# Values of the attention by two half-height matmuls per head, in banks of their own

## The chip, the cores and the metric

The kernel runs on one core of a Trainium2 chip. The metric is the device time of one execution in microseconds (us). A core has TensorE (matrix products, results into PSUM, eight banks of 128 partitions by 512 fp32), VectorE, ScalarE, GpSimd and SyncE (here it only issues DMAs). Each engine runs its own instruction stream in order, and streams wait for each other by semaphores.

## The reference

A decoder layer over x, 16 batches of 64 tokens, 256 wide: layernorm and self-attention, layernorm and cross attention, layernorm and a mixture of experts, each added to x. What matters here is the self-attention, with 16 heads of 128:

```
w = codes * repeat(scales, 32, axis=0)          # for q, k, v and the output
q, k, v = x @ wq + bq, x @ wk + bk, x @ wv + bv  # each (16, 64, 16 heads, 128)
scores  = einsum('bqhd,bkhd->bhqk', q, k) / sqrt(128)
attn    = softmax(scores)
out     = einsum('bhqk,bkhd->bqhd', attn, v) @ wo + bo
```

A batch attends only to itself: 64 queries on 64 keys.

## The kernel before

The 1024 tokens are eight tiles of 128, two batches each. The attention goes through eight head groups c (0 to 7): four heads at a time (hq = c % 4), for four tiles (g = c // 4). `stage_order` writes out one list of steps, `ORDER`, and each engine's program walks it and does its part of each step, so the order on every engine is fixed by hand.

For a head group:

- `scores(c)`: products of 64 queries by 64 keys, into banks 2 and 3. Their stationary operand has 64 columns and the two batches of a tile land in different halves of the partitions (L434).
- `qk(c + 1, h)` for four heads: two results of four matmuls each (L404), q drained by ScalarE, k also by ScalarE but for head 3, which VectorE drains (kT, L914). Between them ScalarE takes the exponential (L724) and VectorE maximum, sums and the product with the inverse sums, which writes the probabilities `Pb`, in a block-diagonal form: batch 0 of a tile in rows and columns 0 to 63, batch 1 in 64 to 127, zeros elsewhere.
- Then for tiles i = 0 to 3, woven into each other: `turn(c, i)` transposes the probabilities of four heads (L447), ScalarE copies them to `PT` (L734); `v(c + 1, i)` makes the V of the next group (L417), drained by ScalarE or VectorE in turns; `values(c, i)` multiplies V and PT (L455); ScalarE copies the result as `OTh` (fp32r, L739), VectorE writes the rest, `OTl` (L965); `outs(c, i)` multiplies both with wo into banks 6 and 7 (L468). The order of TensorE is turn 0, turn 1, v 0, values 0, turn 2, values 1, v 1, outs 0, turn 3, values 2, v 2, outs 1, values 3, v 3, outs 2, outs 3.

After some groups other steps follow: the context's transposes (L478) after group 0, bias and the query-key blocks (L488, L498) after group 3, four transposes of the normalized x and the output blocks (L391 and L392, L509) after group 4. Group 7 has no V of a next group: in its place stand the query weights (`query_weights(m)`, two heads each, L519), drained by ScalarE (`Ah`, L762) and then VectorE (`Al`, L986). The cross attention starts with `rotate(0, 0)` (L534).

Results other than scores and outs take their bank from a ring: `take` gives the next of banks 0, 1, 4, 5 (`ring`, L371) and waits until the last result there is drained. So turn, v, qk, values, context, blocks and query weights share four banks, in the order of TensorE. A values result `pv` is drained by the OTl instruction, and `Banks` keeps a pair of semaphores per bank, full and drained. An fp32 matmul shows as two records in the trace, each with a weight load of its own; one of fp32r or a transpose as one record.

Of the kernel before, what the change touches and what calls it, by code (L numbers as in the profile page):

```python
# [7 lines left out]
ALU = mybir.AluOpType  # L8
ACT = mybir.ActivationFunctionType
# [198 lines left out]
def f32(ap):  # L208
    return ap.bitcast(F)
# [7 lines left out]
def program(nc, x, codes, scl, woc, wos, bq, bk, bv, bo, tabs, cks, tri, kvc, wqr, wkr, kckv, wot, wqx,  # L217
            kcq, wg, w13, w2, out):
    with ExitStack() as ctx:
        def sem(name):  # L220
            return ctx.enter_context(nc.semaphore(name))
# [90 lines left out]
        V = at("V", R3 + 16384, [128, 4, 512])  # L312
        Pb = at("Pb", R3 + 24576, [128, 16, 128])
        PT = [at(f"PT{i}", R3 + 32768 + 2048 * i, [128, 512]) for i in range(2)]
        OTh = [at(f"OTh{i}", R3 + 36864 + 2048 * i, [128, 512], R) for i in range(2)]
        OTl = [at(f"OTl{i}", R3 + 40960 + 2048 * i, [128, 512], R) for i in range(2)]
# [11 lines left out]
        psum = nc.alloc_psum_tensor("psum", [128, 4096], F)  # L328
        ps = Banks(psum, sem)
        y_bank = (4, 5, 6, 7)  # L330

        s_zero, s_ident, s_half, s_kvz, s_pbz = (sem(n) for n in ("zero", "ident", "half", "kv_zero", "pb_zero"))
        d_x, d_cst, d_kvr = [sem("x0_in"), sem("x1_in")], sem("const_in"), sem("kv_in")
# [11 lines left out]
        s_mx, s_exp, s_sum, s_rs = sem("row_max"), sem("exp"), sem("row_sum"), sem("row_inverse")  # L345
        s_pb, s_pb_pool = sem("probs"), sem("probs_by_pool")
        s_ot_hi, s_outs, s_x2, s_xb = sem("ot_hi"), sem("outs"), sem("x2"), sem("x_bias")
        s_kvt, s_kv2 = sem("kv_turned"), sem("kv2")
        s_bv, s_aw_hi = sem("bv_split"), sem("aw_hi")
        s_tt, s_rp_lo, s_rp_hi, s_rp_hi_pool = sem("tt"), sem("rp_lo"), sem("rp_hi"), sem("rp_hi_by_pool")  # L350
# [2 lines left out]
        s_gate, s_route, s_rexp, s_pad = sem("gate"), sem("route"), sem("route_exp"), sem("pad")  # L353
        s_comb = sem("combine")
        s_sl, s_sl2, s_gt_hi, s_down, s_y = sem("silu"), sem("silu2"), sem("gt_hi"), sem("down"), sem("y")

        def wqk(hq, h):
            return (s_wqk_dve, 1 + (h >= 2)) if hq == 0 else (s_wqk_dve, 3) if hq == 1 else (s_wqk_pool, hq - 1)
# [9 lines left out]
        def tensor_program():  # L368
            te = Engine(nc.tensor)
            pe = nc.tensor  # L370
            ring = [0, 0, (0, 1, 4, 5)]  # L371

            def take(*name):
                b = ring[2][ring[0] % len(ring[2])]
                ring[0] += 1
                if b >= 6:
                    te.wait_ge(s_x2, 8)
                ap, n = ps.place(b, *name)
                te.wait_ge(ps.drained[b], n)
                return b, ap  # L380
# [67 lines left out]
                mm.then_inc(ps.full[b], 1)  # L448

            def values(c, i):  # L450
                b, ap = take("pv", c, i)
                te.wait_ge(*ps.emptied("turn", c, i))
                te.wait_ge(*ps.emptied("v", c, i))
                for h in range(4):
                    mm = pe.matmul(ap[:, 128 * h:128 * h + 128], V[:, i, 128 * h:128 * h + 128],  # L455
                                   PT[i % 2][:, 128 * h:128 * h + 128], start=True, stop=True)
                mm.then_inc(ps.full[b], 1)

            def outs(c, i):
                hq = c % 4  # L460
                te.wait_ge(*ps.emptied("pv", c, i))
                te.wait_ge(*wo_(hq))
                if c == 4:
                    te.wait_ge(s_x2, 2 * (i // 2) + 2)
                dst = ps.ap[6 + i // 2][:, 256 * (i % 2):256 * (i % 2) + 256]
                for h in range(4):
                    for n, part in enumerate((OTh, OTl)):
                        mm = pe.matmul(dst, part[i % 2][:, 128 * h:128 * h + 128], wo[:, 4 * hq + h, :],  # L468
                                       start=(hq == 0 and h == 0 and n == 0 and i % 2 == 0),
                                       stop=(hq == 3 and h == 3 and n == 1), skip_group_check=True)  # L470
                mm.then_inc(s_outs, 1)
# [49 lines left out]
                    mm.then_inc(ps.full[b], 1)  # L521

            def rotate(g, j):
                if (g, j) == (0, 4):
                    ring[2] = (0, 1, 4, 5, 6, 7)
                te.wait_ge(*ps.emptied("aw", 15))
                for i in range(4):
                    te.wait_ge(*ps.emptied("xT", 1, 4 * g + i))
                both = take("rot", g, j, 0), take("rot", g, j, 1)
                for half_, (b, ap) in enumerate(both):  # L530
                    n = 0
                    for kt in range(2):
                        for w, xp in ((Ah, xTh), (Ah, xTl), (Al, xTh)):
                            mm = pe.matmul(ap, w[:, kt, half_, 128 * j:128 * j + 128],  # L534
                                           xp[:, kt, 512 * g:512 * g + 512], start=(n == 0), stop=(n == 5))
                            n += 1
                    mm.then_inc(ps.full[b], 1)
# [143 lines left out]
        def scalar_program():  # L681
            sc_ = Engine(nc.scalar)
            act = nc.scalar.activation
# [29 lines left out]
            def v_out(c, i):  # L713
                if i % 2 == 0:
                    sc_.wait_ge(*ps.filled("v", c, i))
                    if c > 0:
                        sc_.wait_ge(*ps.filled("pv", c - 1, i))
                    act(V[:, i, :], ps.of("v", c, i), ACT.Copy).then_inc(ps.drain("v", c, i), 1)

            def exp(c):  # L720
# [5 lines left out]
            def turn(c, i):  # L726
                sc_.wait_ge(*ps.filled("turn", c, i))
                if c == 0:
                    sc_.wait_ge(s_kv2, 2)
                if i >= 2:  # L730
                    sc_.wait_ge(*ps.filled("pv", c, i - 2))
                elif c > 0:
                    sc_.wait_ge(*ps.filled("pv", c - 1, i + 2))
                act(PT[i % 2][:, :], ps.of("turn", c, i), ACT.Copy).then_inc(ps.drain("turn", c, i), 1)  # L734

            def values(c, i):
                sc_.wait_ge(*ps.filled("pv", c, i))
                sc_.wait_ge(s_outs, 4 * c + i - 1)
                act(OTh[i % 2][:, :], ps.of("pv", c, i), ACT.Copy).then_inc(s_ot_hi, 1)  # L739

            def context_turn():
                for q in range(4):
# [108 lines left out]
        def vector_program():  # L851
            ve = Engine(nc.vector)
            tt_, ts_, red = nc.vector.tensor_tensor, nc.vector.tensor_scalar, nc.vector.tensor_reduce
# [63 lines left out]
            def v_out(c, i):  # L917
                if i % 2 == 1:
                    ve.wait_ge(*ps.filled("v", c, i))
                    if c > 0:  # L920
                        ve.wait_ge(*ps.filled("pv", c - 1, i))
                    copy(V[:, i, :], ps.of("v", c, i)).then_inc(ps.drain("v", c, i), 1)

            def less_max(k, *name):
# [37 lines left out]

            def values(c, i):
                ve.wait_ge(s_ot_hi, 4 * c + i + 1)
                tt_(OTl[i % 2][:, :], ps.of("pv", c, i), f32(OTh[i % 2][:, :]),  # L965
                    ALU.subtract).then_inc(ps.drain("pv", c, i), 1)

            def bias():
                ve.wait_ge(d_cst, 96)
# [20 lines left out]
            def rotate(g, j):  # L990
                k = 12 * g + j
                lo, hi = ps.of("rot", g, j, 0), ps.of("rot", g, j, 1)
# [4 lines left out]

                ve.wait_ge(d_cst, 96)
                if k == 0:
                    for i in range(4):  # L1000
                        ve.wait_ge(*ps.filled("pv", 7, i))
                ve.wait_ge(*ps.filled("rot", g, j, 0))
                ve.wait_ge(s_rp_lo, k)
                times(0, lo)
# [442 lines left out]
```

## Time and profile before

| | |
|---|---|
| median of 3 runs | 750.25 us (748.35 to 751.52) |
| profiled execution, its own time | 744.96 us |
| its span | 743.7 us |
| granted TensorE clock, mean | 0.988 |
| TensorE busy | 693.1 us, 93% |
| VectorE busy | 411.5 us, 55% |
| ScalarE busy | 261.5 us, 35% |
| GpSimd busy | 171.3 us, 23% |
| values (L455) on TensorE | 256 records of 276 ns |

A record's duration is longer than its place in the stream, as matmuls are pipelined; what a matmul takes of the engine is read from the distance between starts. The self-attention fills the first 256 us of the span. PE is TensorE's matmul part, PEld its weight loads, DVE VectorE, ACT ScalarE, POOL GpSimd. A granted clock of 1.00 is 2.4 GHz, 0.50 is 1.2 GHz.

### The profile page before, as it was taken

The page shows a single profiled execution, that of the slowest core. Times are in us where ns is not written, and L with a number is a line of the kernel's source. Part 1 is how long each engine was busy: PE and PEld are TensorE (multiplying, and loading weights), DVE is VectorE, ACT ScalarE, POOL GpSimd, SP SyncE. Part 2 cuts the span into 40 slices and gives each one's busy share as a digit, 9 for nine tenths or more (in the row PEclk, how much of TensorE's full clock was granted, in tenths as well). Part 3 has the DMA queues.
Part 4 walks back from the last instruction along what each step waited for, and adds up shares of the span by engine and source line. Part 5 has one row for each costly group of instructions (what it writes and reads, how often), then busy time and mean ns, then how long its engine had stood idle before and what let it go on. Part 6 is the DMA issues. An engine that isn't in the chain of part 4 may idle for free.

```text
span 743.7 us, 11108 instructions
## 1 busy us (share of the span) xinstructions
PE 693.1 (93%) x4516; PEld 602.5 (81%) x4516; DVE 411.5 (55%) x801; ACT 261.5 (35%) x522; POOL 171.3 (23%) x111
## 2 busy tenths in 40 slices
PE   7889899999998999989999968969879999999998
PEld 6778788988887956657667667868769999999997
DVE  3377575273455586765475387675575444434344
ACT  1254354353543401030221232432453453443432
POOL 3536030210001032233241312211322241220200
PEclk9999999999999999999999989999999999999999
DMA  8999030032001200000000022101110311100001
GB/s 270 256 242 244 13 142 2 1 149 77 32 2 49 90 0 1 0 1 1 0 1 1 9 112 81 61 18 44 61 48 27 108 61 61 61 1 1 1 1 58
DMA packets 13764, 44.39 MB, mean 60 GB/s; under 512 B 2193, under 2 KB 2705, under 8 KB 13457
## 3 DMA queue, kind: packets, MB, share of 16 engines
q1 hardware_dynamic: 12704, 42.54, 19.0%
q10 hardware_dynamic: 1008, 1.14, 0.5%
q8 instruction: 36, 0.59, 0.3%
q14 instruction: 16, 0.12, 0.1%
HBM read 42.62 MB, written 1.05 MB: 59 GB/s over the span
## 4 chain that ended last, share of the span: by engine, by line
PE 77%; DVE 14%; DMA 4%; issue 2%; ACT 2%; POOL 1%; SPq 1%; DVEq 0%
PE psum L634 18%; PE psum L662 9%; PE psum L534 7%; PE psum L552 7%; PE psum L404 4%; PE psum L468 4%; PE psum L455 4%; PE psum L596 4%; DMA sclB<-in_scl 4%; PE psum L567 3%; PE psum L417 3%; PE psum L646 3%; PE psum L434 3%; DVE Pb L959 2%; DVE sm L1039 2%
## 5 line engine op out<-in xcount | busy, mean ns | idle before, releaser
L634 PE MATMUL psum<-w13h,xTh 128*128 128x352 f32 x288 | 96.1, 334 | 0.0
L634 PE MATMUL psum<-w13h,xTl 128*128 128x352 f32 x288 | 94.5, 328 | 0.0
L634 PE MATMUL psum<-w13l,xTh 128*128 128x352 f32 x288 | 94.2, 327 | 0.0
L1138 DVE SCALAR_TENSOR_TENSOR gg<-sl,comb,psum 128x176 f32<-128x176 f32 x104 | 41.2, 397 | 83.9 <-ACT sl L833 83.7
L1246 POOL TENSOR_TENSOR w13l<-w13r,w13h 128x1408 fp32r<-128x1408 f32 x13 | 41.8, 3214 | 167.0 <-ACT w13h L816 167.0
L995 DVE TENSOR_TENSOR tt<-psum,tab 128x512 f32<-128x512 f32 x96 | 60.6, 682 | 26.3 <-PE psum L534 25.4
L833 ACT ACTIVATE sl<-psum 128x176 f32<-128x176 f32 x112 | 35.5, 318 | 112.5 <-PE psum L634 112.4
L662 PE MATMUL psum<-w2h,gTh 128*128 128x256 f32 x216 | 67.4, 312 | 6.7 <-DVE gTl L1144 5.6
L662 PE MATMUL psum<-w2h,gTl 128*128 128x256 f32 x216 | 61.3, 284 | 0.0
L662 PE MATMUL psum<-w2l,gTh 128*128 128x256 f32 x216 | 61.3, 284 | 0.0
L552 PE MATMUL psum<-rp,Mb 128*128 128x512 f32 x128 | 58.0, 597 | 0.4 <-DVE rp L1020 0.3
L634 PEld LDWEIGHTS psum<-w13h,xTh 128*128 128x128 f32 x288 | 55.6, 193 | 0.8 <-issue 0.8
L404 PE MATMUL psum<-xTh,W 128*128 128x512 f32 x128 | 52.2, 408 | 4.1 <-DVE W L895 4.0
L634 PEld LDWEIGHTS psum<-w13h,xTl 128*128 128x128 f32 x288 | 55.5, 193 | 0.0
L634 PEld LDWEIGHTS psum<-w13l,xTh 128*128 128x128 f32 x288 | 55.2, 192 | 0.3 <-issue 0.2
L1144 DVE TENSOR_TENSOR gTl<-psum,gTh 128x384 fp32r<-128x384 f32 x72 | 40.0, 556 | 24.7 <-ACT gTh L838 20.8
L1239 POOL TENSOR_TENSOR rp<-tt,tt 128x512 f32<-128x512 f32 x24 | 30.7, 1279 | 96.4 <-DVE tt L995 96.4
L965 DVE TENSOR_TENSOR OTl<-psum,OTh 128x512 fp32r<-128x512 f32 x32 | 22.1, 691 | 53.3 <-ACT OTh L739 53.3
L404 PE MATMUL psum<-xTl,W 128*128 128x512 f32 x128 | 51.2, 400 | 0.0
L662 PEld LDWEIGHTS psum<-w2h,gTh 128*128 128x128 f32 x216 | 41.6, 193 | 7.6 <-DVE gTl L1144 6.3
L552 PEld LDWEIGHTS psum<-rp,Mb 128*128 128x128 f32 x128 | 23.6, 189 | 26.7 <-issue 26.3
L534 PE MATMUL psum<-xTh,Ah 128*128 128x512 f32 x96 | 42.3, 440 | 2.0 <-DVE tt L995 2.0
(156 smaller groups left out, 1525.6 us busy)
## 6 DMA issues: line engine op xcount, KB each, us to landing
w13r<-in_w SPq DMA_DIRECT2D x13, 704.0 KB, 4.1
w2r<-in_w SPq DMA_DIRECT2D x13, 384.0 KB, 3.7
raw<-in_codes SPq DMA_DIRECT2D x4, 1024.0 KB, 18.2
sclB<-in_scl SPq DMA_DIRECT2D x16, 256.0 KB, 10.7
raw<-in_codes SPq DMA_DIRECT2D x4, 512.0 KB, 15.6
sclB<-in_scl SPq DMA_DIRECT2D x16, 128.0 KB, 12.9
wor<-in_woc SPq DMA_DIRECT2D x4, 512.0 KB, 10.8
wob<-in_wos SPq DMA_DIRECT2D x16, 128.0 KB, 12.2
```

The lines of the kernel that those rows point to most:

```text
L404: mm = pe.matmul(ap, W[:, kt, m, 512 * hq + 128 * h:512 * hq + 128 * h + 128], xp[:, kt, 512 * g:512 * g + 512], start=(n == 0), stop=(n = ...
L455: mm = pe.matmul(ap[:, 128 * h:128 * h + 128], V[:, i, 128 * h:128 * h + 128], PT[i % 2][:, 128 * h:128 * h + 128], start=True, stop=True)
L534: mm = pe.matmul(ap, w[:, kt, half_, 128 * j:128 * j + 128], xp[:, kt, 512 * g:512 * g + 512], start=(n == 0), stop=(n == 5))
L552: mm = pe.matmul(ap, Mb[:, 4 * hp + 2 * kk + half_, :], rp[(j0 + kk) % 3][:, half_, :], start=(n == 0), stop=(n == 3))
L634: mm = pe.matmul(ap[:, 0:352], xp[:, kt, 128 * t:128 * t + 128], w[q % 2][:, kt, 352 * u:352 * u + 352], start=(k == 0), stop=(k == 5))
L662: mm = pe.matmul(dst, gp[n % 2][:, 128 * c:128 * c + 128], w[q % 2][:, c, :], start=(n == FIRST_Y[t // 2] and k == 0), stop=(q == LAST_Q[t ...
L833: act(sl[n % 2][:, u, :], src, ACT.Silu).then_inc(s_sl, 1)
L995: return tt_(b3(tt[n][:, :], 64), b3(src, 64), tab[:, j % 3, n, :].unsqueeze(1).to_broadcast([128, 8, 64]), ALU.mult)
L1138: op = stt(out=dst, in0=part_, scalar=(combh if n < 16 else comb)[:, t, e:e + 1], in1=b[:, 176:352], op0=ALU.mult, op1=ALU.mult)
L1144: tt_(gTl[n % 2][:, :], ps.of("gt", n)[:, 0:384], f32(gTh[n % 2][:, :]), ALU.subtract).then_inc(ps.drain("gt", n), 1)
L1239: tt_(o[:, 0, :], tt[0][:, :], tt[1][:, :], ALU.subtract).then_inc(s_rp_lo, 1)
L1246: tt_(w13l[q % 2][:, :, :], w13r[q % 2][:, :, :], f32(w13h[q % 2][:, :, :]), ALU.subtract).then_inc(s_w13, 1)
```

## The change

Each head's product of V and PT is split by batch. As PT is block-diagonal, batch 0 needs only rows 0 to 63 of both operands and columns 0 to 63 of PT, batch 1 the other halves. The new `values` issues for each head two matmuls with 64 rows, 128 stationary columns and 64 moving columns, batch 0 on the upper half of the array's rows into bank 4, batch 1 on the lower half into bank 5: 8 matmuls a tile instead of 4. The four heads of a batch lie side by side in 256 columns of its bank.

Banks 4 and 5 are kept for this. The ring is (0, 1) from the start, and becomes (0, 1, 4, 5) at `rotate(0, 0)`, after all values are drained. Two new semaphores take over for the values: `s_pv` (a tile's values are there) and `s_otl` (its OTl is written). `values(c, i)` waits until the OTl of the tile before is written. OTh and OTl are as before one instruction of 512 elements a partition, which read both banks (`pv_out`) and write in the order head, batch, token (`by_head`).

```diff
+        pv_out = psum[:, 2048:3072].rearrange("p (b c) -> p b c", c=512)[:, :, 0:256].rearrange(
+            "p b (h s) -> p h b s", s=64)
...
+        s_pv, s_otl = sem("values"), sem("ot_lo")
...
+        def by_head(ot):
+            return ot[:, :].rearrange("p (h b s) -> p h b s", b=2, s=64)
...
-            ring = [0, 0, (0, 1, 4, 5)]
+            ring = [0, 0, (0, 1)]
...
             def values(c, i):
-                b, ap = take("pv", c, i)
+                te.wait_ge(s_otl, 4 * c + i)
                 te.wait_ge(*ps.emptied("turn", c, i))
                 te.wait_ge(*ps.emptied("v", c, i))
                 for h in range(4):
-                    mm = pe.matmul(ap[:, 128 * h:128 * h + 128], V[:, i, 128 * h:128 * h + 128],
-                                   PT[i % 2][:, 128 * h:128 * h + 128], start=True, stop=True)
-                mm.then_inc(ps.full[b], 1)
+                    for b in range(2):
+                        lo = 64 * b
+                        mm = pe.matmul(ps.ap[4 + b][:, 64 * h:64 * h + 64], V[lo:lo + 64, i, 128 * h:128 * h + 128],
+                                       PT[i % 2][lo:lo + 64, 128 * h + lo:128 * h + lo + 64], start=True, stop=True)
+                mm.then_inc(s_pv, 1)

             def outs(c, i):
                 hq = c % 4
-                te.wait_ge(*ps.emptied("pv", c, i))
+                te.wait_ge(s_otl, 4 * c + i + 1)
...
             def rotate(g, j):
+                if (g, j) == (0, 0):
+                    ring[2] = (0, 1, 4, 5)
+                    te.wait_ge(s_otl, 32)
...
             def values(c, i):            # ScalarE
-                sc_.wait_ge(*ps.filled("pv", c, i))
+                sc_.wait_ge(s_pv, 4 * c + i + 1)
                 sc_.wait_ge(s_outs, 4 * c + i - 1)
-                act(OTh[i % 2][:, :], ps.of("pv", c, i), ACT.Copy).then_inc(s_ot_hi, 1)
+                act(by_head(OTh[i % 2]), pv_out, ACT.Copy).then_inc(s_ot_hi, 1)
...
             def values(c, i):            # VectorE
                 ve.wait_ge(s_ot_hi, 4 * c + i + 1)
-                tt_(OTl[i % 2][:, :], ps.of("pv", c, i), f32(OTh[i % 2][:, :]),
-                    ALU.subtract).then_inc(ps.drain("pv", c, i), 1)
+                tt_(by_head(OTl[i % 2]), pv_out, f32(by_head(OTh[i % 2])), ALU.subtract).then_inc(s_otl, 1)
```

The other waits on `pv` (of PT's and V's copies, which may not overwrite what a values matmul still reads, and of the first rotate on VectorE) become waits on `s_pv` with the count that stands for the same tile.

## Rows read from the trace of the kernel before

**Rows 1.** Page, part 1: busy time of each engine, share of span, instructions.
```profile
PE 693.1 (93%) x4516; PEld 602.5 (81%) x4516; DVE 411.5 (55%) x801; ACT 261.5 (35%) x522; POOL 171.3 (23%) x111
```

**Rows 2.** Windows: stretch, length, busy us by engine, clock; groups 3 and 7.
```profile
116.20:140.40 24.20, 24.20 (x194) 21.96 (x194) 12.92 (x23) 11.63 (x21) 0.00 (x0) 1.00 0.00 1
228.60:256.30 27.70, 24.09 (x209) 23.16 (x209) 16.48 (x30) 13.23 (x26) 3.09 (x2) 1.00 0.19 67
```

**Rows 3.** Timeline of TensorE, group 3: start, duration, engine, line, operation, idle before.
```profile
127.37 1.04 PE L447 MATMUL psum<-ident,Pb 128*128 128x128 f32 x8
128.16 0.48 PE L417 MATMUL psum<-W,xTh 128*128 128x512 f32 x1
...
129.18 1.05 PE L455 MATMUL psum<-PT,V 128*128 128x128 f32 x8
130.07 0.60 PE L447 MATMUL psum<-ident,Pb 128*128 128x128 f32 x4
130.51 1.06 PE L455 MATMUL psum<-PT,V 128*128 128x128 f32 x8
131.41 0.50 PE L417 MATMUL psum<-W,xTh 128*128 128x512 f32 x1
```

**Rows 4.** Waits of TensorE, 20 to 256 us: total, times, longest.
```profile
PE psum L455 <- DVE kT L914: 3.4, 3, 2.1
```

**Rows 5.** Timeline of TensorE around scores, group 3's start and group 4's end.
```profile
116.01 0.27 PE L392 MATMUL psum<-ident,xh 128*128 128x128 f32 x1
116.21 0.50 PE L434 MATMUL psum<-kT,qT 128*64 128x64 f32 x5
...
154.61 0.40 PE L434 MATMUL psum<-kT,qT 128*64 128x64 f32 x4
154.94 0.51 PE L404 MATMUL psum<-xTh,W 128*128 128x512 f32 x1
155.28 0.40 PE L404 MATMUL psum<-xTl,W 128*128 128x512 f32 x1
155.52 0.40 PE L404 MATMUL psum<-xTh,W 128*128 128x512 f32 x1
```

**Rows 6.** Timeline of TensorE's weight loads behind the scores of group 4.
```profile
154.94 0.19 PEld L404 LDWEIGHTS psum<-xTh,W 128*128 128x128 f32 x1
155.04 0.19 PEld L404 LDWEIGHTS psum<-xTl,W 128*128 128x128 f32 x1
```

**Rows 7.** Timeline after group 4: output blocks and next scores; VectorE's xTl.
```profile
176.70 3.67 PE L509 MATMUL psum<-Fo,Fk 128*64 128x256 f32 x32 [0.28 <-DVE xTl L884]
180.21 0.28 PE L434 MATMUL psum<-kT,qT 128*64 128x64 f32 x2
...
176.22 1.41 DVE L884 TENSOR_TENSOR xTl<-psum,xTh 128x256 fp32r<-128x256 f32 x4 [1.57 <-ACT xTh L697]
```

**Rows 8.** Timelines of VectorE and ScalarE beside rows 3.
```profile
128.06 0.75 DVE L914 TENSOR_SCALAR kT<-psum,bks 128x512 f32<-128x512 f32 x1
130.90 0.69 DVE L965 TENSOR_TENSOR OTl<-psum,OTh 128x512 fp32r<-128x512 f32 x1 [2.09 <-ACT OTh L739]
...
130.27 0.60 ACT L739 ACTIVATE OTh<-psum 128x512 fp32r<-128x512 f32 x1 [1.18 <-PE psum L455]
```

**Rows 9.** Timeline of ScalarE, group 4: the third result of qk drained.
```profile
158.73 0.68 ACT L706 ACTIVATE qT<-psum,bqs 128x512 f32<-128x512 f32 x1
```

**Rows 10.** Timelines in group 7: TensorE, then VectorE (from 226 us).
```profile
240.02 1.57 PE L519 MATMUL psum<-Akc,Aq 128*128 128x192 f32 x8 [2.47 <-DVE Al L986]
241.42 1.04 PE L447 MATMUL psum<-ident,Pb 128*128 128x128 f32 x8
...
239.42 3.29 DVE L986 TENSOR_TENSOR Al<-psum,Ah 128x384 fp32r<-128x384 f32 x6
```

**Rows 11.** Windows of the cross attention: clock behind a stretch of idle TensorE.
```profile
433.00:439.70 6.70, 3.02 (x20) 2.76 (x20) 5.08 (x11) 3.93 (x8) 2.00 (x1) 1.00 0.01 3
439.70:446.50 6.80, 4.96 (x19) 4.99 (x20) 6.46 (x18) 1.41 (x3) 1.15 (x1) 0.50 0.01 4
```

More of the change, by code:

```diff
@@ L716, in v_out @@
                     if c > 0:
-                        sc_.wait_ge(*ps.filled("pv", c - 1, i))
+                        sc_.wait_ge(s_pv, 4 * c + i - 3)
                     act(V[:, i, :], ps.of("v", c, i), ACT.Copy).then_inc(ps.drain("v", c, i), 1)
@@ L730, in turn @@
                 if i >= 2:
-                    sc_.wait_ge(*ps.filled("pv", c, i - 2))
+                    sc_.wait_ge(s_pv, 4 * c + i - 1)
                 elif c > 0:
-                    sc_.wait_ge(*ps.filled("pv", c - 1, i + 2))
+                    sc_.wait_ge(s_pv, 4 * c + i - 1)
                 act(PT[i % 2][:, :], ps.of("turn", c, i), ACT.Copy).then_inc(ps.drain("turn", c, i), 1)
             def values(c, i):
-                sc_.wait_ge(*ps.filled("pv", c, i))
+                sc_.wait_ge(s_pv, 4 * c + i + 1)
                 sc_.wait_ge(s_outs, 4 * c + i - 1)
-                act(OTh[i % 2][:, :], ps.of("pv", c, i), ACT.Copy).then_inc(s_ot_hi, 1)
+                act(by_head(OTh[i % 2]), pv_out, ACT.Copy).then_inc(s_ot_hi, 1)
             def context_turn():
@@ L920, in v_out @@
                     if c > 0:
-                        ve.wait_ge(*ps.filled("pv", c - 1, i))
+                        ve.wait_ge(s_pv, 4 * c + i - 3)
                     copy(V[:, i, :], ps.of("v", c, i)).then_inc(ps.drain("v", c, i), 1)
@@ L999, in rotate @@
                 if k == 0:
-                    for i in range(4):
-                        ve.wait_ge(*ps.filled("pv", 7, i))
+                    ve.wait_ge(s_pv, 32)
                 ve.wait_ge(*ps.filled("rot", g, j, 0))
```

## The prediction

> **What bounds the kernel now.** I read the engine table of the page first: TensorE is busy 693 of 743.7 us, and no other engine comes to 60% [rows 1]. An average hides stages, so I cut the attention into the stretches between two score stages. In the stretch of head group 3 TensorE is busy for the whole 24.20 us, VectorE for half of it; in the last stretch (group 7, with the query weights) it is busy 24.09 of 27.70 us and VectorE and ScalarE set the pace [rows 2]. So what TensorE must do or wait for in groups 0 to 6 is path, nearly without cover. Third, the order of TensorE's own work around the change: turns, V, values, turn, values, V, each starting where the last one stops [rows 3]. Fourth, what it waits for: the values wait 3.4 us in 3 groups for kT, which shares their ring bank [rows 4].
>
> **The change, part by part.**
>
> *The matmuls.* Before, a tile takes 8 records of values (4 fp32 matmuls, two records each): 130.51 to 131.41, 0.90 us, or 112 ns each [rows 3]. After, there are 8 matmuls, 16 records, each with half the rows and 64 moving columns instead of 128. What a record costs is the larger of its weight load and its moving pass. The scores stream 64 columns at a spacing of 57 ns (the four last records of the stretch) [rows 5]. A load of 128 columns that finds the array free is followed by the next after 0.10 us [rows 6]. The new load still has 128 columns, so a record can't go below some 0.108 us, unless two loads run at once. Whether two of them on different halves of the rows do, no row shows. The nearest rows are the output blocks, whose matmuls alternate between two halves of the columns: 32 records of 256 moving columns in 3.51 us, 0.22 us a pair [rows 7]; alone, such a record would take twice the 0.108 us that 128 fp32 columns take. So pairs overlap fully there, loads too. I take the same for halves of the rows: 8 pairs of 0.108 us are 0.86 us against 0.90, a gain of 0.03 x 32 tiles = 1.0 us. The other end is no overlap, 16 x 0.108 = 1.73 us, a loss of 0.83 x 32 = 26.6 us. The best end is a pair in the time of a scores record, 8 x 0.057 = 0.46 us, a gain of 0.44 x 32 = 14 us.
> The Trainium skill ("TensorE: Matmul & The Clock Gate", LDWEIGHTS) says that a load's time goes by its columns and not by the rows in use; by that rule, halving the rows saves nothing, and only overlap keeps the loads from doubling.
>
> *Entering and leaving the split array.* Around the scores, the only matmuls of half width in this stage, the trace shows what a change of shape costs. Into it: 0.20 us between starts (116.01 to 116.21) where such transposes follow at 0.11 [rows 5], 0.09 more. Out of it: from the last record (154.61 + 3 x 0.057 = 154.78) to 154.94 is 0.16 us against 0.057, 0.10 more; then 0.34 against 0.235 until the next, 0.10 more, because its load could not be made ahead [rows 5, 6]. Going in, the first 128-column load is bare as well, 0.10. An excursion so costs 0.39 us; the old values paid at most 0.1 of such a gap, and not everywhere; I take 0.38. Bounds: 0 if splitting rows is free, 0.4 if as here. Each of 32 tiles is one excursion: 25 in full (9.5 us); in groups 0 to 6 the first tile pays only 0.09, as its way out lies inside the wait costed below (0.6 us). Together 10.1 us.
> The Trainium skill ("TensorEngine Tiling (Array Packing)", Key Properties) states that changing the tiling mode, not just the tile, drains TensorE. The trace agrees in sign, with the 0.09 and 0.10 us above; this rule speaks against the change.
>
> *The ring of two banks.* Banks 4 and 5 leave the ring, so from the start to the first rotate a result goes to bank 0 or 1 and must be drained before the second next.
> - kT and the second turn. The order is ..., q of head 3, k of head 3, turn 0, turn 1: turn 1 now takes kT's bank, where before it was the first values, after V. kT is drained by VectorE behind the probabilities, at 128.06 + 0.75 = 128.81 [rows 8]. Turn 1 starts at 128.87, then 0.44 us of transposes and 1.02 of V (128.16 to 129.18 [rows 3]): values start at 130.33 instead of 129.18, 1.15 late, in four groups (3 to 6). In groups 0 to 2 the old values already waited for kT [rows 4], so nothing of turn 1 and V (0.44 + 0.94) is covered any more: 1.4 each. 4 x 1.15 + 3 x 1.4 = 8.8 us. Queued behind the waiting turn on TensorE are V and the values, and ScalarE and VectorE wait for these.
> - q and k of the next group: groups of 4 matmuls each 0.93 us. ScalarE drains in 0.69 and just keeps up, but it holds the third result until both exponentials are out (158.73 + 0.68 = 159.41 [rows 9]), and TensorE would write that bank at 154.94 + 4 x 0.93 = 158.66: 0.75 late. 0.45 of it disappears in the wait for kT; 0.3 x 4 groups = 1.2 us. (Groups 0 to 2 are bound by kT anyway.)
> - Elsewhere: context turn, the four xT turns (xTl alone takes VectorE 1.41 us [rows 7], and a third turn waits for the first xTl) and the output and key blocks. 2.0 us, between 0 and 4.
>
> *The values' own banks.* The values of tile i+1 wait for OTl of tile i. In group 3, OTl is done at 130.90 + 0.69 = 131.59, 2.41 us after its values began [rows 3, 8]; with a bare load and a semaphore's way 2.55. The second values began 1.33 us after the first (129.18 to 130.51). So 1.2 us of wait, in 7 groups: 8.4 us. Tiles 2 and 3 come 2.8 us or more after the one before and just escape. In group 7 query weights lie between the first two, and this wait is nothing.
>
> *Group 7.* Query weights take a bank per head. Before, four results fit ahead of the probabilities; now two, and each later pair waits for Al. VectorE runs six Al from 239.42 in one go while TensorE resumes at 240.02 [rows 10]; with two banks TensorE, ScalarE and VectorE take turns, some 1.1 to 2 us a pair, and turn 0 waits for the seventh Al: by my count at 244.05 instead of 241.42, 2.6 late, and turn 2 another 0.7. 3.3 us, bounds 1 and 5.
>
> *The clock.* A stretch in which TensorE was busy 3.02 of 6.70 us was followed by one at half clock (0.50, the 1.2 GHz level) for 6.80 us [rows 11]. The idle places of group 7 now come near that. I add 1.7 us (3.4 us at half rate); bounds 0 and 3.4.
>
> *ScalarE's and VectorE's copies* keep 512 elements a row and one instruction each (0.60 and 0.69 us [rows 8]); read over two banks in runs of 64 I cost them at nothing, bounds 0 and 0.1 us each.
>
> *Sum.* -1.0 + 10.1 + 8.8 + 1.2 + 2.0 + 8.4 + 3.3 + 1.7 = 34.5 us. Groups 0 to 2 run beside the loads of weights and GpSimd's products, and a later TensorE finds these further on: I take 2 us off (0 to 4). That is 32.5 us on the profiled execution's own 744.96 us, 777.5. The runs shown have a median of 750.25, 5.3 above that one; on it, the same difference gives 782.8, and I say 782.
>
> **The rivals.**
> - *The halves don't overlap* (the change does not do what it says). Speaking for it: no row has two row halves; against: the column halves. The tile takes 1.73 us instead of 0.86, on the path: 27.6 us more, 810.
> - *Cheap split.* Rows split without a change of shape, and the waits partly covered: without the 10.1 us and with 4 us less of ring waits, 768. Against it: the scores' rows.
> - *Faster.* A pair goes at the pace of the scores, 0.057 us, at 14 us gained, shapes change free, and the ring's waits of groups 0 to 2 fall into weight loads. It begins where the tile's gain exceeds the waits: with 14 gained, no more than 10 may remain of the 25.4 us of waits (8.8 + 1.2 + 2.0 + 8.4 + 3.3 and 1.7 of clock). At 10 left the time is 746. Against it: the spacing of bare loads [rows 6] and TensorE without a gap to hide in [rows 2].
> - *No change*, a mixture of these near 750.
>
> **How the numbers follow.** Forecast 0.65, no overlap 0.17, cheap split 0.10, faster 0.04, no change 0.04. 0.5% (3.8 us) is about what a measurement tells from none. Faster 0.04, same 0.04, slower 0.92. The likeliest case has its own range of 770 to 795; the range is 765 to 812, which takes in no overlap and nearly all of the cheap split.
>
> **What would show it.** Right: 16 records of values per tile, starting within some 10 ns of each other two by two, 0.11 us a pair; 0.09 us and more around them; a new wait of the turns (L447) for kT of 1 us a group; a new wait of the values for OTl of about 1 us, once a group; stretches of groups 3, 5 and 6 near 28 us instead of 24.2; nothing changed from the rotates on. Wrong: values of 1.7 us (no overlap) or 0.5 us (loads faster than the bare ones); no wait for OTl, which would mean that the ring had been the limit before; or ScalarE's copy well above 0.60 us.

## The result, and the profile after

The changed kernel takes 779.95 us (median of 4 runs, 775.17 to 785.03) against 749.74 us of the kernel before beside it: a ratio of 1.040, 95% interval 1.033 to 1.048. The forecast was 782, within 765 to 812. The profiled execution took 775.17 us with a span of 773.9, 30.2 us more than the one of before.

The page's first part, answering to [rows 1]: TensorE has 20 us more to do by its own records, and 10 us more in which it stands still.

```profile
PE 713.2 (92%) x4772; PEld 603.8 (78%) x4772; DVE 409.1 (53%) x801; ACT 265.4 (34%) x522; POOL 171.4 (22%) x111
```

Windows of the kernel after, answering to [rows 2]: the start up to the first scores, group 5 (as group 3, but with no blocks behind it), group 7, and the stretch of half clock in it. Columns: stretch, length, busy us of PE, PEld, DVE, ACT, POOL, clock, DMA.

```profile
0.00:32.10 32.10, 25.22 (x116) 19.92 (x116) 12.74 (x26) 8.78 (x14) 17.72 (x18) 0.89 0.96 262
196.99:224.87 27.88, 26.36 (x226) 21.62 (x223) 11.90 (x19) 12.01 (x20) 0.00 (x0) 1.00 0.20 72
252.83:286.40 33.57, 27.42 (x241) 24.58 (x241) 17.04 (x30) 13.67 (x26) 3.09 (x2) 0.95 0.16 55
265.60:269.00 3.40, 2.92 (x10) 2.42 (x8) 1.58 (x3) 1.06 (x3) 0.00 (x0) 0.50 0.04 14
```

TensorE no longer fills group 5: 27.88 us, 1.52 of them idle, where it had 24.18 without a gap. The rest, from the first rotate on, takes 487.4 us against 487.3: the whole difference lies in the self-attention.

TensorE in group 3, answering to [rows 3]. Here transposes are L453, V L423, values L463.

```profile
136.12 0.66 PE L453 MATMUL psum<-ident,Pb 128*128 128x128 f32 x4
137.10 0.66 PE L453 MATMUL psum<-ident,Pb 128*128 128x128 f32 x4 [0.33 <-DVE kT L925]
137.51 0.48 PE L423 MATMUL psum<-W,xTh 128*128 128x512 f32 x1
...
138.62 1.11 PE L463 MATMUL psum<-PT,V 64*128 64x64 f32 x16
139.66 0.66 PE L453 MATMUL psum<-ident,Pb 128*128 128x128 f32 x4
141.15 1.11 PE L463 MATMUL psum<-PT,V 64*128 64x64 f32 x16 [0.84 <-DVE OTl L976]
142.19 0.50 PE L423 MATMUL psum<-W,xTh 128*128 128x512 f32 x1
142.53 0.40 PE L423 MATMUL psum<-W,xTl 128*128 128x512 f32 x1
```

Sixteen records take 1.04 us up to the next V where eight took 0.90. The pairs are real. A window of 0.1 us at the second values holds two weight loads and two matmuls, each pair merged into one row that begins at 141.15:

```profile
141.15 0.19 PEld L463 LDWEIGHTS psum<-PT,V 64*128 64x128 f32 x2 [1.07 <-DVE OTl L976]
```
```profile
141.15 0.33 PE L463 MATMUL psum<-PT,V 64*128 64x64 f32 x2 [0.84 <-DVE OTl L976]
```

In the trace's nanoseconds the two starts are 7 apart, the next pair comes 160 later (its load was bare) and each further pair 112 after the last: as much as one full-height record before. So the pairs gained nothing at all, and the change of shape is paid on top. The first part of the price stands in the stage that follows: the first record of V starts 0.20 us after the last pair, where before it came 0.12 us after the last record. The two places where the path stands still are also in these rows: turn 1 waits for kT, the second values for OTl.

The waits of TensorE up to 290 us, answering to [rows 4] (total, times, longest):

```profile
PE psum L463 <- DVE OTl L976: 5.8, 7, 0.8
PE psum L527 <- DVE Al L996: 5.0, 3, 2.5
PE psum L410 <- ACT qT L717: 4.7, 7, 1.7
PE psum L410 <- DVE W L906: 3.7, 1, 3.7
PE psum L453 <- DVE kT L925: 2.8, 7, 0.7
PE psum L397 <- DVE xTl L895: 1.6, 2, 0.9
```

Seven waits for OTl (one a group, not in group 7), seven for qT in the matmuls of q and k, and seven for kT. Why kT is late shows in VectorE's row beside the ones of group 3: it begins 0.55 us after VectorE was free, on the release of a matmul of k. It is the filling that is late, not VectorE. The second row is the OTl that ends at 141.10; the second values start 0.05 us later.

```profile
136.30 0.75 DVE L925 TENSOR_SCALAR kT<-psum,bks 128x512 f32<-128x512 f32 x1 [0.55 <-PE psum L410]
140.41 0.69 DVE L976 TENSOR_TENSOR OTl<-psum,OTh 128x512 fp32r<-128x512 f32 x1 [3.36 <-ACT OTh L750]
```

Group 7, answering to [rows 10]: the query weights come two heads at a time, each time behind Al, and turn 0 starts at 269.14, 16.3 us after its scores instead of 12.8 (241.42 after 228.61).

```profile
260.20 1.57 PE L527 MATMUL psum<-Akc,Aq 128*128 128x192 f32 x8 [2.10 <-DVE Al L996]
264.24 1.61 PE L527 MATMUL psum<-Akc,Aq 128*128 128x192 f32 x8 [2.46 <-DVE Al L996]
266.33 2.88 PE L527 MATMUL psum<-Akc,Aq 128*128 128x192 f32 x8 [0.48 <-DVE Al L996]
269.14 0.66 PE L453 MATMUL psum<-ident,Pb 128*128 128x128 f32 x4
```

The lengths below are worked out from the starts of the score stages in the timelines (group 7 up to the first rotate), in us. They carry most of what follows: groups 5 and 6 hold nothing but the attention, away from weight loads, and where neither has a star they agree to 0.1 us. A star marks a stretch with 3.4 us or more of half clock in it.

| kernel | before scores | 0 | 1 | 2 | 3 | 4 | 5 | 6 | 7 |
|---|---|---|---|---|---|---|---|---|---|
| before | 29.35* | 32.58 | 28.74 | 25.55 | 35.03 | 28.96 | 24.18 | 24.23 | 27.73 |
| after | 32.10* | 33.27 | 28.79 | 29.77 | 38.97 | 34.09 | 27.88 | 27.96 | 33.60* |
| ring_only | 32.51* | 30.72 | 32.83* | 27.64 | 36.88 | 32.01 | 25.82 | 25.84 | 32.24* |
| ring_and_one_bank | 35.20* | 32.34 | 32.45* | 28.79 | 38.02 | 33.12 | 26.93 | 26.98 | 32.58* |
| halves_two_pairs | 32.78* | 33.10 | 32.82* | 28.87 | 38.06 | 33.21 | 26.97 | 27.01 | 33.64* |
| halves_ring4 | 29.19* | 32.26 | 26.75 | 27.14 | 37.11 | 31.04 | 26.26 | 26.31 | 28.82 |
| full_height_64 | 33.02* | 35.86 | 30.94 | 32.32 | 41.52 | 38.19* | 30.46 | 30.49 | 34.80 |
| halves_in_order | 33.77* | 34.45 | 31.95* | 33.24* | 42.47* | 36.08 | 31.39* | 33.00* | 35.49* |
| kt_by_scalare | 29.22 | 39.50* | 28.47 | 31.39* | 39.03 | 34.11 | 27.91 | 27.99 | 32.40 |
| exp_later | 29.33* | 39.48* | 28.50 | 28.55 | 40.59* | 34.18 | 27.99 | 29.55* | 33.38* |
| full_banks23 | 29.40* | 32.03* | 29.23* | 24.96 | 34.92 | 28.85 | 24.07 | 24.12 | 28.96* |
| banks23_kt_by_scalare | 27.93 | 33.58* | 26.95 | 24.93 | 34.92 | 28.85 | 24.07 | 24.13 | 27.72 |

The 2.75 us by which the stretch ahead of the first scores grew are mostly not the change's. VectorE dequantizes the first weights W when their scales have landed (the row's wait for `sclB`), before and after:

```profile
14.29 2.36 DVE L895 TENSOR_TENSOR W<-raw,sclB 128x1024 fp32r<-128x1024 f32 x2 [3.44 <-DMA sclB<-in_scl]
16.19 2.36 DVE L906 TENSOR_TENSOR W<-raw,sclB 128x1024 fp32r<-128x1024 f32 x2 [4.71 <-DMA sclB<-in_scl]
```

The load came 1.90 us later in this execution, and the first matmul of q starts 1.90 us later with it (17.56 against 15.66); ring_only, with the same ring, has this row at 14.27. The change doesn't touch these loads. The stretch also holds 3.4 us more of half clock, some 1.7 us at half rate.

### The profile page after: what moved, and what is told of

The parts are those of the page before. It is cut to its first block, busy times and chain, and to the rows that moved or that the text cites. A ratio compares the mean times of both kernels' runs of the same rounds, so it can differ in the third digit from the quotient of the medians.

```text
span 773.9 us, 11618 instructions
## 1 busy us (share of the span) xinstructions
PE 713.2 (92%) x4772; PEld 603.8 (78%) x4772; DVE 409.1 (53%) x801; ACT 265.4 (34%) x522; POOL 171.4 (22%) x111
## 4 chain that ended last, share of the span: by engine, by line
PE 78%; DVE 11%; ACT 4%; DMA 4%; issue 2%; POOL 1%; SPq 0%; DVEq 0%
PE psum L645 17%; PE psum L673 9%; PE psum L563 7%; PE psum L545 7%; PE psum L410 5%; PE psum L463 4%; PE psum L476 4%; PE psum L423 4%; PE psum L607 4%; DMA sclB<-in_scl 4%; PE psum L578 3%; PE psum L657 3%; PE psum L440 3%; DVE sm L1048 2%; PE psum L598 2%
## 5 line engine op out<-in xcount | busy, mean ns | idle before, releaser
L410 PE MATMUL psum<-xTh,W 128*128 128x512 f32 x128 | 55.4, 433 | 8.4 <-ACT qT L717 4.7
```

What stands on the lines that cost most here:

```text
L410: mm = pe.matmul(ap, W[:, kt, m, 512 * hq + 128 * h:512 * hq + 128 * h + 128], xp[:, kt, 512 * g:512 * g + 512], start=(n == 0), stop=(n = ...
```

## The experiments

The change has three parts that can be had alone: the ring of two, values that wait for the OTl of the tile before, and the split. The first four experiments build them up in other combinations.

**ring_only.** The kernel before, and in `values`:

```diff
-            ring = [0, 0, (0, 1, 4, 5)]
+            ring = [0, 0, (0, 1)]              # (0, 1, 4, 5) from rotate(0, 0) on
...
-                b, ap = take("pv", c, i)
+                b = 4 + i % 2
+                ap, n = ps.place(b, "pv", c, i)
+                te.wait_ge(ps.drained[b], n)
```

> The ring alone: the values stay four full-height matmuls a tile, written to bank 4 (even tiles) or 5 (odd tiles), which are out of the ring of two, as in the changed kernel. No split, and no wait for the OTl of the tile before. Theory (ring, values' banks and split each cost their own share of the 30 us): 30 less about 8 for the OTl wait and 10 for the split, so about 12 above the kernel before, 762 us (758 to 766); turn 1 waits for kT in each group, group 7 is some 4 us longer, and values follow at 0.112 us a record with nothing bare around them. Rival (the split array is the loss): 750 to 753. Rival (the ring is the loss): 778 to 780.

Measured: 763.17 us against 747.20 of the kernel before, ratio 1.021 (1.016 to 1.026). Group 5, by its window:

```profile
192.60:218.41 25.81, 25.12 (x194) 21.42 (x191) 11.89 (x19) 11.90 (x20) 0.00 (x0) 1.00 0.23 77
```

1.63 us more than before in groups 5 and 6 each, 4.5 in group 7 (with 3.4 us of half clock that the kernel before doesn't have there), and 3.2 ahead of the first scores. TensorE's wait list has one of 3.1 us in V before the scores, for kT, that the kernel before had at 0.5. So the ring alone is about half of the loss (16 of some 30 us), more than the 12 expected: the time fell into the expected range because the kernel before took 747 us beside this run, not 750. Both rivals are out.

**ring_and_one_bank.** As ring_only with `b = 4`: the second part on top, still without the split.

> As ring_only (four full-height matmuls a tile, ring of two), but every tile's values go to bank 4, so they wait for the OTl of the tile before, as in the changed kernel. Theory: the three shares add up, so the wait that is worth 0.92 us a group with the halves (27.9 against 27.0 in groups 5 and 6) is worth as much without them: 25.8 + 0.9 to 1.1 in groups 5 and 6, seven groups, 770 us against 763. Rival (OTl comes late only because the halves start and end slowly): 25.8 to 26.0, 763 to 765.

Measured: 771.22 us, ratio 1.032 (1.027 to 1.037).

```profile
199.93:226.86 26.93, 25.27 (x194) 21.36 (x191) 11.91 (x19) 11.99 (x20) 0.00 (x0) 1.00 0.21 74
```

The wait for OTl is worth 1.12 us a group with full-height values, as the theory had it.

**halves_two_pairs.** The changed kernel with two pairs of banks for the values:

```diff
-                te.wait_ge(s_otl, 4 * c + i)
+                te.wait_ge(s_otl, 4 * c + i - 1)
+                first = 4 - 2 * (i % 2)
...
-                        mm = pe.matmul(ps.ap[4 + b][:, 64 * h:64 * h + 64], ...
+                        mm = pe.matmul(ps.ap[first + b][:, 64 * h:64 * h + 64], ...
```

> The changed kernel with a second pair of banks for the values: odd tiles write banks 2 and 3, which the scores leave idle then, even tiles 4 and 5, so values wait for the OTl of two tiles before. Ring of two and split stay. Theory: the first gap of the groups 0 to 6 goes (0.84 us of wait in group 3's trace, about 1.1 with what it hides), but the way out of the split array that lay in it now costs 0.2: 6 to 8 us less than the changed kernel, about 773 us. Rival (the OTl wait only moves to the next wait, for turns or V): within 2 us of the changed kernel, 778 to 780.

Measured: 774.79 us, ratio 1.037 (1.031 to 1.043), and group 5:

```profile
198.84:225.80 26.96, 26.30 (x226) 21.63 (x223) 11.90 (x19) 12.00 (x20) 0.00 (x0) 1.00 0.21 74
```

The wait for OTl is gone from the list, and with it 0.92 us of group 5. In the run's total the difference is 5.2 us by the medians where 6 to 8 were expected, and the intervals of the two ratios overlap: this run was not beside one of the changed kernel. Against ring_only, which has the same ring and no OTl wait, groups 5 and 6 are 1.15 us longer: the whole price of the split, 0.29 us a tile. It can be added up from starts. In group 5 of both traces, four distances per tile: from the record ahead of the values into them, from their first start to their last, from there to the next stage, and on to its second record. The halves make these longer by 0.37, 0.22, 0.52 and 0.09 us over four tiles, 1.20 in all.

**halves_ring4.** The split alone, in banks 2 and 3, which the softmax has read by then and the next scores don't need yet:

```diff
-            ring = [0, 0, (0, 1)]
+            ring = [0, 0, (0, 1, 4, 5)]
...
-        pv_out = psum[:, 2048:3072] ...
+        pv_out = psum[:, 1024:2048] ...
-                        mm = pe.matmul(ps.ap[4 + b] ...
+                        mm = pe.matmul(ps.ap[2 + b] ...
```

> The split alone: the halves write banks 2 and 3, idle between the scores, and the ring keeps its four banks 0, 1, 4, 5. The values still wait for the OTl of the tile before. Theory: split (about 10) and OTl wait (about 8), nothing of the ring: 750 + 18 = 768 us (764 to 771). Rival (the ring is nearly all of the loss): 752 to 757. Rival (the split is nearly all): 776 to 780.

Measured: 757.91 us, ratio 1.016 (1.011 to 1.020): 10.7 us above the kernel before beside it, less than the 18 expected and below the expected range, and more than the rival's.

```profile
183.49:209.75 26.26, 25.42 (x226) 22.04 (x223) 11.90 (x19) 11.78 (x20) 0.00 (x0) 1.00 0.22 76
```

Groups 5 and 6 are 2.08 us longer than before. With the ring's 1.63 that makes 3.71, and the changed kernel shows 3.70 and 3.73: here the parts add up. They don't in groups 0 and 1, where halves_ring4 is not longer than the kernel before at all (-0.32 and -1.99). I had multiplied a steady group's price by seven and eight. Added up over the runs, 16.0 us for the ring and 10.7 for the rest are 26.7 of some 30.

**full_height_64.** The changed kernel without the row slices:

```diff
-                        mm = pe.matmul(..., V[lo:lo + 64, i, 128 * h:128 * h + 128],
-                                       PT[i % 2][lo:lo + 64, 128 * h + lo:128 * h + lo + 64], ...
+                        mm = pe.matmul(..., V[:, i, 128 * h:128 * h + 128],
+                                       PT[i % 2][:, 128 * h + lo:128 * h + lo + 64], ...
```

> Eight matmuls a tile as in the changed kernel, 64 moving columns each and into banks 4 and 5, but of full height: all 128 rows of V and of PT, whose other half is zeros. The shape of the array never changes. Against the kernel with the halves in order (16 records one after another too) it differs in nothing but the change of shape. Theory: the 16 records take 1.75 to 1.8 us a tile, and the change of shape is worth 0.29 us a tile (ring_only against halves_two_pairs: 25.83 against 26.98 us in groups 5 and 6, by 4 tiles): group 5 takes 31.4 - 1.2 = 30.2 us and the run 791 us (787 to 795). Rival (going in and out costs nothing, the 0.29 is something of the pairs): group 5 at 31.4 us, 799 us.

Measured: 798.79 us (2 runs), ratio 1.070 (1.063 to 1.076), and a tile's values:

```profile
150.03 2.00 PE L463 MATMUL psum<-PT,V 128*128 128x64 f32 x16 [0.96 <-DVE OTl L976]
151.84 0.48 PE L423 MATMUL psum<-W,xTh 128*128 128x512 f32 x1
```

1.81 us for 16 records, 0.112 us each, with only 64 columns to stream: as long as a record of 128 columns. The scores stream 64 columns too, behind weight loads of 64 columns, every 0.058 us. So a weight load of 128 columns sets the pace, and half the moving columns are worth nothing.

The comparison that the run was made for fails. It took 31.4 us as the length of group 5 in halves_in_order, which holds 3.4 us of half clock there and, as that run's text shows, does not take its records one after another. So the group's 30.46 us being near the theory's 30.2 supports nothing, and neither does the run's total, which hit the rival's 799. What the run does show of the change of shape stands at the edges of a tile that waits for nothing, the third of group 5, here and in the changed kernel:

```profile
233.48 0.60 PE L453 MATMUL psum<-ident,Pb 128*128 128x128 f32 x4
233.92 1.90 PE L463 MATMUL psum<-PT,V 128*128 128x64 f32 x16
```
```profile
217.17 0.60 PE L453 MATMUL psum<-ident,Pb 128*128 128x128 f32 x4
217.70 1.11 PE L463 MATMUL psum<-PT,V 64*128 64x64 f32 x16
```

From the last of the four transposes to the first record of values it is 0.11 us at full height and 0.20 with halves; from the first record (or pair) to the next 0.06 against 0.16; from the last to V 0.085 against 0.20. These three edges make 0.31 us, with the same number of records and of columns on both sides: so it is the halves that cost the 0.29, and not the number of matmuls.

**halves_in_order.** The two loops exchanged:

```diff
-                for h in range(4):
-                    for b in range(2):
+                for b in range(2):
+                    for h in range(4):
```

> The changed kernel with the two loops over heads and batches exchanged: a tile does four matmuls of batch 0 on the upper rows, then four of batch 1 on the lower, the same 16 records. Theory (what keeps a tile at 0.9 us is that neighbours stand on different halves, loads included): the runs of one half follow at 0.108 to 0.112 us a record, 1.75 us a tile, 0.85 x 32 = 27 us more than the changed kernel, about 807 us. Rival (the array takes waiting instructions of the other half ahead of their turn, so that the order does not matter): 778 to 783 us, pairs as before.

Measured: 800.60 us (2 runs), ratio 1.072 (1.067 to 1.078), between the theory and the rival. A tile in group 4:

```profile
190.58 1.60 PE L463 MATMUL psum<-PT,V 64*128 64x64 f32 x16
192.11 0.66 PE L453 MATMUL psum<-ident,Pb 128*128 128x128 f32 x4
```

1.53 us to the next stage instead of 1.04, not the 1.8 that a strict order would take. In the trace's nanoseconds five records start at 0.16 and then 0.11 us, the next one 6 ns behind the fifth, after which starts alternate in steps of 0.05, and the last four stand alone again. The trace doesn't say which record belongs to which half, but the starts fall into two chains, each 0.16 and then 0.11 us apart throughout, the second begun 6 ns behind the fifth record of the first; and the record that begins it lasts 320 ns like the very first, the others 272. So the array takes up the second half's work while some of the first half's still waits. The other tiles without half clock show the same. Group 4, the last without half clock, is 1.99 us longer than in the changed kernel, four tiles of 0.50; the run also has half clock in six of its groups, where the changed kernel has it in one.

**kt_by_scalare.** The changed kernel with `if h < 3` taken away in ScalarE's `qk` and VectorE's part of it dropped.

> The changed kernel with k of head 3 drained by ScalarE instead of VectorE. The prediction said that turn 1 is 1.15 us late because VectorE gets to kT only after the probabilities. Its trace speaks against that: kT starts 0.4 us after its last matmul, so the filling is late and not VectorE. If the prediction's step holds: groups 3 to 6 each 1 us shorter, groups 0 to 2 up to 1.4, some 8 us less, 770 us. If it is the filling (theory now): groups 5 and 6 within 0.1 us of 27.9, groups 0 to 2 together 0 to 3 us less, 775 to 779 us.

Measured: 779.52 us, ratio 1.045 (1.040 to 1.050): no gain over the changed kernel's 1.040 (1.033 to 1.048). Group 5:

```profile
201.70:229.61 27.91, 26.46 (x226) 21.66 (x223) 11.16 (x18) 12.58 (x21) 0.00 (x0) 1.00 0.21 72
```

It is where it was, 27.91 against 27.88. Turn 1 still waits for kT, with ScalarE as the releaser:

```profile
PE psum L453 <- ACT kT L720: 2.0, 7, 0.3
```

So in a steady group VectorE does not make kT late, and a step of the prediction falls. On groups 0 to 2, which were to take 0 to 3 us less, the run says nothing: they take 7.5 us more than in the changed kernel, and hold 13.6 us of half clock where that has none.

**exp_later.** The same, and in `stage_order`:

```diff
-            yield from [("scores", c), ("qk", c + 1, 0), ("exp", c), ("qk", c + 1, 1), ("probs", c)]
+            yield from [("scores", c), ("qk", c + 1, 0), ("qk", c + 1, 1), ("exp", c), ("probs", c)]
```

> The kernel before this one, and ScalarE takes the exponential one head later, behind q and k of head 1, in groups 1 to 6. Theory (ScalarE holds the third result behind the exponential, TensorE then stands 0.7 us and more before it can go on, and this is most of what the ring of two costs in a group): q and k run at 0.93 us each, turn 0 starts 11.2 us after the scores instead of 12.2, and groups 3, 5 and 6 lose 1.0 to 1.4 us of their 27.9, the probabilities just in time; some 5 us less than kt_by_scalare. Rival (the probabilities were no less urgent): turn 0 or turn 2 then waits for Pb, and the groups stay at 27.9 or grow.

Measured: 780.53 us, ratio 1.045 (1.041 to 1.050), no gain either; group 5 is 27.99 us. ScalarE's timeline there says why:

```profile
208.49 0.69 ACT L720 ACTIVATE kT<-psum,bks 128x512 f32<-128x512 f32 x1 [0.24 <-PE psum L410]
209.07 1.14 ACT L734 ACTIVATE sm<-sm 128x512 f32<-128x512 f32 x2
210.11 0.68 ACT L717 ACTIVATE qT<-psum,bqs 128x512 f32<-128x512 f32 x1
```

Wherever the two exponentials stand, they hold ScalarE for 1.1 us among drains that come every 0.93 us, and with two banks the result behind them is drained late. In this kernel it is the fifth instead of the third that ScalarE drains late, and TensorE's one long step between two results of q and k moves with it, from the one before the fifth (1.44 us in kt_by_scalare, group 5) to the one before the seventh (1.50). Turn 0 comes 12.20 us after the scores as against 12.11. The rival's reason (that the probabilities would be late) was not what happened: no wait for Pb came up in this group. Theory and rival were both wrong on how, the rival right on how much.

**full_banks23.** What the table suggests: banks 2 and 3 are free when values are made, so let the full-height values have them, one each in turn, and leave the ring of four to the rest.

```diff
-                b, ap = take("pv", c, i)
+                b = 2 + i % 2
+                ap, n = ps.place(b, "pv", c, i)
+                te.wait_ge(ps.drained[b], n)
```

> The kernel before, with its full-height values, but written to bank 2 (even tiles) or 3 (odd tiles), which are idle between the softmax's read of the scores and the next scores. The ring keeps 0, 1, 4, 5 and has four results a group less to carry. Theory: the wait of the values for kT in groups 0 to 2 goes (3.4 us in the trace), all else stays; as groups 0 and 1 run beside weight loads, 1 to 3 us of it show: 0.2 to 0.4% less than the kernel before. Rival (those groups are set by loads and GpSimd): no difference, within 0.1%.

Measured: 740.73 us (11 runs) against 747.22 (16), ratio 0.9926 (0.9892 to 0.9960). It is 0.7% faster than the kernel before (0.4 to 1.1), where 0.2 to 0.4 were expected, and so faster than the changed one. Its waits of TensorE up to 300 us have kT once:

```profile
PE psum L404 <- DVE W L897: 5.3, 2, 3.1
PE psum L521 <- DVE Al L988: 3.3, 2, 2.5
PE psum L447 <- DVE kT L916: 2.9, 1, 2.9
```

Groups 2 to 6 are each 0.1 to 0.6 us shorter. That makes 1.0 us; the other 4.5 of the ratio don't show in the profiled execution, whose span is 743.3, no better than that of the kernel before (743.7), at a mean clock of 0.979 against 0.988. That execution took 745.03 us, the longest of the eleven. It holds three stretches of half clock, of 3.4 us each and with TensorE busy throughout, in groups 0, 1 and 7, where the kernel before has none; at half rate these are some 5.1 us (an estimate), enough to hide the rest. Nor is all of the gain surely the banks': three of the sixteen runs of the kernel before took 740.0 to 741.0 us at mean clocks of 0.988 to 0.991, as short as this kernel's median. So the gain is measured and only 1.0 us of it located.

**banks23_kt_by_scalare.** That kernel with kT by ScalarE.

> full_banks23 with k of head 3 drained by ScalarE instead of VectorE. What full_banks23 still waits for in the attention is kT, once, for 2.9 us (now turn 2 of group 0), behind the slow probabilities beside GpSimd. Theory: this wait goes and VectorE has 0.75 us less to do a group; as group 0 runs beside the weight loads, 0 to 2 us of it show: 0 to 0.3% less than full_banks23's 0.9926 of the kernel before. Rival (ScalarE, with all eight drains of q and k, comes late to PT of tile 0): groups 5 and 6 grow by 0.3 us or more, and the run is slower than full_banks23.

Measured: 740.54 us (8 runs) against 747.10 (13), ratio 0.9896 (0.9856 to 0.9935). It is the fastest run here, but the interval overlaps that of full_banks23, so the second edit's own share is not settled. Group 5 is 24.07 us in both, which excludes the rival, and the wait for kT is gone from the list, though turn now waits 2.2 us for Pb:

```profile
PE psum L404 <- DVE W L896: 6.2, 2, 3.7
PE psum L521 <- DVE Al L987: 3.3, 2, 2.5
PE psum L447 <- DVE Pb L960: 2.2, 1, 2.2
```

## Why the prediction was right, point by point

The direction, the size (30.2 us measured on the profiled executions, 32.5 forecast) and the three causes held: each costs about what a steady group was priced at. Part of the size is luck: groups 0 to 2 grew by 4.2 us less than priced, and 2.75 us came from a stretch priced at nothing, most of them from a load that landed later. Of the terms:

- *The matmuls* (1.0 us gained by pairs of 0.108 us). Pairs overlap, loads included, 7 ns apart. They come every 0.112 us and not every 0.108, so the gain was nothing. full_height_64 shows that a load of 128 columns is what holds a record there, as the bare loads [rows 6] had said; this also excludes the best end of 0.46 us. That halves of the rows overlap like halves of the columns was taken over without a row to show it, with 0.17 set against it; it came true. The Trainium skill ("TensorE: Matmul & The Clock Gate", LDWEIGHTS) has a load's time go by its columns whatever the rows in use, and the trace agrees: 0.112 us from load to load on a half of 64 rows as at 128.
- *In and out of the split array* (0.38 us a tile). 0.29 by halves_two_pairs against ring_only. Going in was sized right, 0.09 us. The bare load behind it cost 0.05 and not 0.10, as the spans of the values differ by 0.055 (0.836 against 0.78). Going out cost 0.08 or 0.09 on two tiles as priced, and 0.17 on the two whose V had followed the old values by only 0.03. The term that wasn't there is the last, 0.10 until the second record of the next stage: it is 0.33 behind V's first, but the kernel before pays the same there.

```profile
131.41 0.50 PE L417 MATMUL psum<-W,xTh 128*128 128x512 f32 x1
131.74 0.40 PE L417 MATMUL psum<-W,xTl 128*128 128x512 f32 x1
```

The Trainium skill ("TensorEngine Tiling (Array Packing)", Key Properties) announces that TensorE drains at a change of tiling mode. The trace agrees in sign, with 0.29 us a tile in all; that a drain is what takes this time, no run shows.
- *The wait for OTl* (1.2 us a group, seven groups). 0.92 us with the halves, 1.12 without. Near; it is the one that the waits list shows seven times, 5.8 us.
- *kT and turn 1* (8.8 us) and *q and k* (1.2 us). The sum of both for a steady group was 1.45, and ring_only measures 1.63. The division is wrong, and so is the reason given for the larger part: "kT is drained by VectorE behind the probabilities". The step that failed is that q and k would be 0.75 us late and 0.45 of it disappear in a wait for kT that VectorE sets, 1.15 us long. In fact turn 0 comes 12.19 us after the scores of group 3 instead of 11.16, so q and k lose 1.03 us in full: about 0.5 where the fifth result needs the bank of the third, and some 0.1 at most others, where a matmul that had to wait for its bank has its load made late (it starts with its matmul at 129.68, and the next record follows after 0.34 us instead of 0.23). kT is then filled so late that VectorE is already free, and turn 1 waits only 0.33 us, not the 1 us named as a sign; with its bare load it starts 0.5 us later than it would behind turn 0. 1.03 and 0.5 are nearly the 1.63. kt_by_scalare confirms it. That the sum came out with a wrong division is luck.
- *Groups 0 to 2.* Priced at 3.7 us each with 2 us off for weight loads, 9.1 in all; measured 0.7, 0.05 and 4.2. The stretch ahead of the first scores, priced at nothing, grew by 2.75: 1.90 from the later load of the scales, the rest within what 3.4 us more of half clock make. The ring has a price there too, but another execution shows it: in ring_only V of group 0 waits 3.1 us for kT, in the changed kernel's profile it doesn't.
- *The copies* (nothing). OTh takes 0.60 us and OTl 0.69 in both traces, so reading over two banks in runs of 64 is free, as priced.
- *Group 7* (3.3 us, 1.7 for the clock, four excursions of 0.38; 6.5 in all). 5.87 measured. The stretch of half clock came where I expected it, at 265.60 for 3.40 us, behind the waits for Al of 2.10 and 2.46 us. Whether it comes is not the ring's alone: kt_by_scalare and full_height_64 have the same ring and none in group 7, and full_banks23 has the ring of four and 3.4 us.
- *Elsewhere* (2.0 us). Behind group 4, 34.09 - 28.96 = 5.13, of which a steady group explains 3.7: 1.4 are left for the four xT turns and the output blocks. Behind group 3 only 0.2, so 1.6 against 2.0.

By place: 2.75 + 0.7 + 0.05 + 4.2 + 3.9 + 5.1 + 3.7 + 3.7 + 5.9 = 30.0, and 0.1 for the rest of the kernel.

## What to carry to other kernels

Splitting a matmul by rows into two that run side by side saves nothing when a weight load and not the moving columns sets its pace: look at the smallest distance between two loads of that width before counting columns. Banks that are set apart are paid for by everything else in the ring. A ring hides the time that a result waits for its drain only as far as its banks reach: with two banks and a result every 0.93 us, one stretch of 1.1 us in which the draining engine did something else was enough to stall TensorE, and with four it was not. Look first for banks whose contents are dead at that point, as the scores' two were here.

## What was not expected of the hardware

By the starts in its trace, the array works on the other half of its rows out of the written order, but not at once. With four matmuls of one half ahead of four of the other, 16 records took 1.33 us from first start to last, against 0.84 in alternation and 1.73 at full height; the second half began 6 ns behind the fifth record of the first. Alternating in the program is worth 0.50 us a tile.
